# Nine of 49 first-stage products move into the edge steps, and the gathers start from normalised rows

## What is computed

```python
xn = layernorm(x)
support = segment_sum(edge_weight[:, None] * xn[src], dst)       # one sum per row
x = x + (support @ gnn_weight + gnn_bias) + linear_attention(xn) # k, v, q of xn, 8 heads
x = x + ffn(layernorm(x))                                        # gated, a mean over all rows, last norm
```

## Time and profile before

| | |
|---|---|
| median of 3 runs | 1573.97 us |
| the profiled execution's own time | 1572.78 us |
| its span, first to last instruction | 1570.8 us |
| first gather starts | 203.46 us |
| last of 784 gathers starts | 1200.69 us |
| last stage begins (its first statistics) | 1210.01 us |
| busy share of the span: PE, DVE, ACT, POOL (page, part 1) | 86%, 63%, 41%, 56% |
| mean granted clock of TensorE | 0.949 |

### The profile page before, as it was taken

How to read it: one execution, slowest core, us unless ns; L and a number is a source line. 1 busy time by engine, 2 the same in 40 slices (tenths; PEclk the granted TensorE clock), 3 DMA queues, 4 the chain that set the end, 5 groups by cost and what they waited for, 6 DMA issues and landing times. The chain is left out here.

```text
span 1570.8 us, 25004 instructions
## 1 busy us (share of the span) xinstructions
PE 1352.6 (86%) x7963; PEld 612.1 (39%) x7963; DVE 983.2 (63%) x2019; ACT 646.6 (41%) x1045; POOL 875.8 (56%) x908
## 2 busy tenths in 40 slices
PE   4989978989888897997888988899897799889994
PEld 2544423333333333443333434433343244464441
DVE  7978733334434444486756657777797777266887
ACT  4787722222222222132323323333343466327774
POOL 1000367777777777677777777777774000016763
PEclk9999989999999999899989999999999799989997
DMA  6989778888888889677777777778775988633442
GB/s 218 312 299 346 259 233 269 273 262 275 262 265 261 279 266 309 177 244 230 237 230 237 235 231 237 229 234 261 230 237 149 247 204 216 168 134 126 175 174 100
DMA packets 201552, 366.46 MB, mean 233 GB/s; under 512 B 77100, under 2 KB 82878, under 8 KB 201440
## 3 DMA queue, kind: packets, MB, share of 16 engines
q0 software_dynamic: 62720, 205.57, 42.8%
q1 hardware_dynamic: 138000, 158.43, 31.4%
q10 hardware_dynamic: 720, 1.06, 0.2%
HBM read 287.93 MB, written 65.38 MB: 225 GB/s over the span
## 5 line engine op out<-in xcount | busy, mean ns | idle before, releaser
L1167 POOL DMA_INDIRECT rows<-y_rows,idxT x516 | 495.7, 961 | 176.1 <-issue 166.6
L919 ACT ACTIVATE mb<-bank,ones,ncols 128x512 f32<-128x512 f32 x98 | 76.3, 779 | 439.2 <-PE bank L1979 439.2
L1535 DVE SCALAR_TENSOR_TENSOR acc<-bank,maskt,acc 128x512 f32 x196 | 138.0, 746 | 108.5 <-PE bank L2087 89.0
L2075 PE MATMUL bank<-rows,hots 128*32 128x512 f16 x1548 | 118.3, 413 | 67.4 <-DMA rows<-y_rows,idxT 64.6
L1979 PE MATMUL bank<-Wg,xtb 128*128 128x512 f16 x588 | 139.0, 388 | 15.6 <-DVE xtb L1469 7.9
L1979 PE MATMUL bank<-ztg,G 128*128 128x512 f16 (+1 forms) x624 | 133.5, 377 | 15.4 <-DMA ztg<-zhigh 15.1
L1979 PE MATMUL bank<-KVP,qT 128*128 128x512 f16 x588 | 143.7, 397 | 0.0
L1979 PE MATMUL bank<-Wk,xta 128*128 128x512 f16 x588 | 139.4, 388 | 0.0
L1979 PE MATMUL bank<-Wq,xta 128*128 128x512 f16 x588 | 137.2, 384 | 0.0
L2059 PE MATMUL bank<-xr,kh 128*128 128x512 f16 x392 | 124.2, 400 | 2.3 <-DVE kl L1562 2.3
L1555 DVE SCALAR_TENSOR_TENSOR kf<-bank,cols,mb 128x512 f32<-128x512 f32 x49 | 36.7, 749 | 134.3 <-ACT mb L922 134.3
(11 more groups left out here) (316 smaller groups left out, 2425.6 us busy)
## 6 DMA issues: line engine op xcount, KB each, us to landing
xta<-xt_rows SPq DMA_DIRECT2D x98, 256.0 KB, 4.1
x_rows<-xhl SPq DMA_DIRECT2D x49, 256.0 KB, 3.6
xt_rows<-xtb SPq DMA_DIRECT2D x49, 256.0 KB, 3.7
y_rows<-yb SPq DMA_DIRECT2D x49, 256.0 KB, 3.5
xr<-x_rows SPq DMA_DIRECT2D x49, 256.0 KB, 4.0
zt_rows<-ztg SPq DMA_DIRECT2D x49, 256.0 KB, 2.3
acc<-in_x SPq DMA_DIRECT2D x48, 256.0 KB, 4.1
xd<-zt_rows SPq DMA_DIRECT2D x12, 1024.0 KB, 5.5
```

What stands on the lines that cost most here:

```text
L919: nc.scalar.activation(mb[:, :], of[:, :], ACT.Relu, scale=ncols[:, col:col + 1], bias=ones[:, 0:1]).then_inc(f_min, 1)
L1167: pool.indirect_dma_start(out=row_slot(s, k).rearrange("p a d -> p (a d)"), out_offset=None, in_=y_rows, in_offset=bass.IndirectOffsetOnAx ...
L1535: nc.vector.scalar_tensor_tensor(out=flat(acc, tile + m), in0=edge_bank(n)[:, :], scalar=maskt[:, m, n:n + 1], in1=flat(acc, tile + m), op ...
L2075: ins = nc.tensor.matmul(edge_bank(n)[W * k:W * k + W, :], hots[:, r, p, :, hot_column(s, k)], row_slot(s, k)[:, q, :], start=s == FIRST[n ...
```

## The change

1. **Nine y products move.** `EARLY` is tiles 6 to 45: their 40 products stay in the head, one tick later than before (tick t+3, and their splitting in tick t+5 instead of t+3). The products of tiles 0 to 5 and 46 to 48 are made from `xt_rows`, loaded back into `xta`, in slots -6 to 0 (`Y_FIRST` = -6): two each in slots -6 and -1, one in each of the others. PE runs eight of them before its part of slot 0. They have two buffers `ylate` and four banks.
2. **The first group gathers normalised rows.** `XG` = 1: the 16 slots of group 0 gather from `x_rows`; the sum is turned instead of placed, split (`agg_higher`, `agg_lower`) and multiplied with `Wg16` (`weigh`, 12 matmuls). POOL waits before slot 0 for x_rows, xt_rows and the 40 early y stores, and for all y stores only before slot 16.
3. **Homes.** `xtb` has four buffers instead of two. `rows_v` goes: `xr`, `kh`, `kl` lie there now, since `Wg16` must live longer. `rows_p` lies over the raw `Wq`, which is now split in slots 8 to 10, so it opens only at slot 16 (`PLACES_AT`). Gathered rows have 3 homes for slots 0 to 15 and 4 up to `TURN` - 7, where there were 5.
4. **Weights.** The largest value, scale and split of `gnn_w` move from ahead of tick 0 to ticks 1, 3 and 5 to 7; the splits of `Wk` and `Wq` move out of ticks 38 to 42 into slots -4 to -2 and 8 to 10. `pack_edges` moves from ticks 33 to 39 to the loads of k tiles 8 to 14.
5. **The attention's places.** k starts in slot 3 (before -2), `TURN` is 86 (81), q starts in slot 91 (86) and takes 6 tiles in 12 slots (13), so that the last q product is in slot 187 (190). `GATE_AT` stays 165.

The core of the diff:

```diff
+G_LARGEST_AT, G_SCALE_AT, G_HIGH_AT, G_LOW_AT = 1, 3, 5, 6
-K_FIRST, K_NUM, K_DEN = -2, 10, 6
+XG = 1
+XSTEPS = sum(LONG[:XG])
+AGG = 2.0 ** -27
+PLACES_AT, WEIGHTS_AT = 16, (-4, 8)
+EARLY = list(range(6, 46))
+Y_ORDER = EARLY + [t for t in range(T) if t not in EARLY]
+NEARLY, NLATE = len(EARLY), T - len(EARLY)
+Y_FIRST, Y_NUM, Y_DEN, Y_BANKS = -6, 5, 6, 4
+K_FIRST, K_NUM, K_DEN = 3, 10, 6
-Q_FIRST, Q_NUM, Q_DEN = TURN + 5, 13, 6
+Q_FIRST, Q_NUM, Q_DEN = TURN + 5, 12, 6
...
 def row_homes():
-    free, homes = list(range(RING + 2)), []
+    free, homes = list(range(RING)), []
     for s in range(NGR):
+        if s == PLACES_AT:
+            free.insert(0, RING)
...
-            sp.wait_ge(bias_spread, 16 * 3)
-            sp.wait_ge(q_spread, 16 * 3)
+            head_ticks(head_stores, T + 2)
+            for i in range(4):
+                sp.wait_ge(head.turned_kept[i], 16 * ((T + 3 - i) // 4))
...
             def load_turned(n, t):
                 b = n % 2
-                at_least(sp, f_done, n - 1)
+                if n > 1:
+                    sp.wait_ge(y_made, min(NEARLY + n - 1, T))
+                at_least(sp, f_done, n - NLATE - 1)
...
+            for i in range(NEARLY, T + 2):
+                if i < T:
+                    load_turned(i - NEARLY, Y_ORDER[i])
+                if i >= NEARLY + 2:
+                    keep_y(i - 2)
...
-            pool.wait_ge(edges_packed, 16 * 7)
             head_kept(pool)
-            pool.wait_ge(y_made, T)
             for s in range(NGR):
+                if s == XSTEPS:
+                    for b in range(2):
+                        pool.wait_ge(y_kept[b], 16 * ((T + 1 - b) // 2))
...
+            def y_product(i):
+                n = i - NEARLY
+                b = n % 2
+                pe.wait_ge(xt_in[b], 16 * (n // 2) + 16)
+                at_least(pe, y_low, max(NEARLY, i - Y_BANKS + 1))
+                accumulate(y_bank(i)[:, :], [(xta[:, b, p, c, :], Wg16[:, q, c, :]) for c in range(C) for p, q in PASSES]
+                           ).then_inc(y_made, 1)
...
                 if s != NGR - 1:
                     place(s - 1)
                 else:
                     part(s)
+                weigh(s - 3)
+                for t in y_slots(s):
+                    y_product(t)
```

More of the change, by code:

```diff
@@ L67 @@
 U_HOT = 4
-H_HIGH, H_LOW = 3 + 2 * C, 2 + 2 * C
+H_HIGH, H_LOW = 3 + 2 * C, 3 + 2 * C
 OUTSIDE = float(1 << 20)
@@ L104, in row_homes @@
         home = free.pop(0)
-        while home in (RING, RING + 1) and s >= KEYS_END or home == RING + 3 and s >= GATE_AT:
+        while home == RING and s >= KEYS_END or home == RING + 3 and s >= GATE_AT:
             home = free.pop(0)
@@ L377, in __init__ @@
                     self.turned_in = [sem(f"{name}_turned_in{b}") for b in range(2)]
-                self.turned_kept = [sem(f"{name}_turned_kept{b}") for b in range(2)]
+                self.turned_kept = [sem(f"{name}_turned_kept{b}") for b in range(4 if name == "head" else 2)]
                 self.six = sem(name + "_six")
@@ L467, in exists, with y_slots, y_bank, y_home @@
             return not isinstance(g, int) or 0 <= tile_at(g, j) < T
+        def y_slots(s):
+            return [NEARLY + i for i in range(NLATE) if Y_FIRST + Y_NUM * i // Y_DEN == s]
+        def y_bank(i):
+            return bank[4 + i % 2] if i < NEARLY else bank[i % Y_BANKS]
+        def y_home(i):
+            return (yearly if i < NEARLY else ylate)[:, i % 2]
+        def early_at(at):
+            return EARLY.index(at) if at in EARLY else None
+        def early_before(t):
+            return sum(e <= t for e in EARLY)
         def k_slot(t):
@@ L487, in head_kept @@
         def head_kept(eng):
-            for b in range(2):
-                n = 16 * ((T + 1 - b) // 2)
-                eng.wait_ge(head.turned_kept[b], n)
-                eng.wait_ge(y_kept[b], n)
             for i in range(4):
+                eng.wait_ge(head.turned_kept[i], 16 * ((T + 3 - i) // 4))
                 eng.wait_ge(x_kept[i], 16 * ((T + 3 - i) // 4))
+            for i in range(2):
+                eng.wait_ge(y_kept[i], 16 * ((NEARLY + 1 - i) // 2))
         def late(g, j):
@@ L872, in head_tick @@
                     act.wait_ge(head.turned, t + 1)
-                    at_least(act, y_made, t - 1)
-                    at_least(act, head.turned_kept[1], 16 * half_at(g1, j1))
-                    nc.scalar.copy(xtb[:, 1], turned16(7)).then_inc(odd_out, 1)
+                    at_least(act, head.turned_kept[t % 4], 16 * (t // 4))
+                    at_least(act, y_made, early_before(t - 4))
+                    nc.scalar.copy(xtb[:, t % 4], turned16(7)).then_inc(odd_out, 1)
                 at = tile_at(g, j)
@@ L957, in kv_rows @@
                                          ).then_inc(kvp_out, 1)
-            act.wait_ge(y_low, T)
+            act.wait_ge(head.low, T)
             act.wait_ge(pool_set, 22)
-            for s in range(K_FIRST, SLOTS_END):
+            for s in range(Y_FIRST, SLOTS_END):
+                for t in y_slots(s - 1):
+                    y_higher(t)
+                if s == WEIGHTS_AT[0]:
+                    weight_high(1, Wk16, Wkraw)
+                if s == WEIGHTS_AT[1]:
+                    weight_high(2, Wq16, Wqraw)
+                n = ending(s - 2)
+                if n is not None and n < XG:
+                    agg_higher(n)
                 for slot_of, after, work in ((k_slot, 1, k_feature), (q_slot, 1, q_feature), (k_slot, 2, k_higher),
@@ L1550, in k_whole @@
                 b = t % 2
+                if t < 2:
+                    for i in range(2):
+                        dve.wait_ge(y_kept[i], 16 * ((T + 1 - i) // 2))
                 dve.wait_ge(f_exp, t + 1)
@@ L1688, in _ @@
             dve.wait_ge(pool_set, 22)
-            for s in range(K_FIRST, SLOTS_END):
-                n = ending(s - 2)
-                if n is not None:
+            for s in range(Y_FIRST, SLOTS_END):
+                for t in y_slots(s - 1):
+                    y_lower(t)
+                for k, w16, raw in ((1, Wk16, Wkraw), (2, Wq16, Wqraw)):
+                    if WEIGHTS_AT[k - 1] < s <= WEIGHTS_AT[k - 1] + 2:
+                        weight_low(k, w16, raw, low_made, s - WEIGHTS_AT[k - 1] - 1, 2)
+                n = ending(s - 2)
+                if n is not None and n < XG:
+                    agg_lower(n)
+                if n is not None and n >= XG:
+                    add_group(n, tile_at_group(n))
+                n = ending(s - 5)
+                if n is not None and n < XG:
                     add_group(n, tile_at_group(n))
```

227 lines of the change are left out of this document (129 added, 98 removed).

## The result

The changed kernel took 1582.85 us, the median of 20 runs (1576.32 to 1589.19), beside 1571.59 us for the kernel before in the same series (20 runs): a ratio of 1.0067, 95% interval 1.0052 to 1.0081. It is slower, by some 11 us. A second series of the same kernel gave 1.0051 (1.0031 to 1.0070). My 1575 us named the likeliest case as "nothing measurable"; the time lies inside the range of 1563 to 1586, and what came is nearest to the rival in which the head gains little. The profiled execution of the changed kernel took 1589.19 us (span 1587.4), the highest of its runs, so its trace shows more loss than the medians do.

A forecast was written before the change was run, and what follows sets the result against it. POOL's gather issue was taken to bound the edge steps, no single engine the head. From 1572.8 us, -15.6 (head) + 14.7 (first wait) + 0.5 + 0.5 + 2.0 = +2.1 gave 1574.9, predicted as 1575 us, range 1563 to 1586.

The forecast's parts named there:

- nothing measurable: Likeliest case for the whole kernel: the head's gain becomes POOL's wait for the first home, both some 15 us; chance 0.41.
- the rival in which the head gains little: Head: later ticks keep 3.5 us each, so the gain is 8 us instead of 15.6, total 1582 us; chance 0.16.
- What bounds the kernel: Edge steps: POOL's gather issue, 1.25 us apart, sets the pace and cannot make up for a wait; no single engine limits the head.
- Part 1, ticks 0 to 11: Start of the head: DVE's edge-list wait and load keep the gain small, 3 us at tile 11.
- After tile 48's low part: End of the head up to the first gather: 9.3 us instead of 14.1, a gain of 4.8 us.
- Part 1, ticks 11 to 48: Main part of the head: 3.35 us a tick instead of 3.56, 7.8 us gained, ends 2 and 16.
- Part 2, POOL's first wait: Before the 13th gather: eight y products delay PE's part of slot 0, costing 14.7 us; bounds 10 and 22.
- Part 3: Behind the first wait: 0.5 us in slots 3 to 15, 0.5 for repacking, 2.0 for the q stage, `TURN` unchanged.
- the late-q rival: From slot 165 on: PE at 95% of POOL's pace makes POOL wait 9 to 10 us, total 1583; chance 0.17.
- `TURN`: Around that slot: homes, key products and waits keep their places to one another, so POOL's 6.4 us wait stays.
- The weighing: Whole kernel, chances: nothing measurable 0.41, faster 0.26, late q 0.17, small head gain 0.16.
- the signs I had named: First gather at 184 to 191, one 10 to 20 us wait before the 13th, no `xtb` store waits, `TURN` wait 6 us.

The follow-up runs named there:

- experiment 2: Changed kernel with the late y products spread over slots -2 to 3, four instead of eight before slot 0, k and all behind three slots later; 1567.65 us, 0.9984.
- Experiment 1: Changed kernel with the split of y one tick after its product instead of two; 1578.66 us, ratio 1.0045.
- experiment 4: Changed kernel with both edits: split of y one tick after its product, and late y products in slots -2 to 3; 1563.09 us, ratio 0.9957.
- experiment 9: Kernel of experiment 4 with four buffers instead of two for the split y of the head; 1562.41 us, ratio 0.9922.
- experiment 10: Kernel of experiment 9 with four banks instead of two for the products of tiles 22 to 45; 1557.23 us, ratio 0.9904.
- experiment 8: Kernel before with the q pace alone changed, 6 tiles in 12 slots instead of 13; 1575.46 us, ratio 1.0011.
- experiment 7: Changed kernel with four banks instead of two for the products of tiles 22 to 45, split of y left two ticks behind; 1581.04 us, ratio 1.0043.
- experiment 6: Kernel of experiment 5 with twelve late y products instead of nine (tiles 43 to 45 late too), k one slot later; 1574.05 us, ratio 0.9993.
- Experiment 3: Kernel before with the changed kernel's homes alone: three for slots 0 to 15, a fourth from slot 16; 1573.47 us, ratio 1.0008.
- experiment 5: Kernel of experiment 4 with the late y products one slot later, slots -1 to 4, two before slot 0; 1565.43 us, ratio 0.9933.

## Why the prediction was partly right

Where the time went, by stretches between gathers, from two traces of each kernel:

| stretch | before | changed | difference of means | predicted |
|---|---|---|---|---|
| to the first gather | 203.5, 204.8 | 195.2, 195.2 | -8.9 | -15.6 |
| first to 13th gather | 15.4, 15.5 | 29.5, 30.4 | +14.5 | +14.7 |
| 13th to 57th (slots 3 to 13) | 56.8, 56.6 | 59.3, 57.3 | +1.6 | +0.5 |
| 57th to 337th (k stage) | 358.3, 362.2 | 360.8, 359.4 | -0.1 | +0.5 |
| 337th to 393rd (around `TURN`) | 76.6, 72.9 | 82.2, 83.2 | +8.0 | 0 |
| 393rd to the last (q stage) | 490.3, 491.4 | 489.6, 490.5 | -0.9 | +2.0 |
| last gather to the end | 370.1, 367.6 | 370.9, 366.7 | 0.0 | 0 |

The two spans differ by 14.2 us in the mean of these traces, by 16.6 in the first two, and the medians by 11.3 and 8.5 us.

- **What bounds the kernel** was right. POOL's gathers follow each other at 1.25 us in every kernel here, and none made up for a wait: 8.9 us more or less before the 13th gather (experiment 2) is at least that much at the end.
- **Part 1, ticks 0 to 11**: 4.5 us gained for 3 predicted. **After tile 48's low part**: 3.9 for 4.8. Both near. (The four pieces of the second add up to 9.0 us, not to the 9.3 used; measured were 10.2.)
- **Part 1, ticks 11 to 48: the step that failed.** I took 3.35 us a tick, between the old pace and PE's floor, and 7.8 us gained; measured 3.57 and nothing. I counted each engine's load and the buffers that the change adds, and not the tick more that it puts between the product and its split while the product's banks stay two. Experiment 1 gave 5.1 us for that tick alone; on experiment 4 four buffers for y gave 2.2 more (experiment 9), and four banks from tile 22 on another 1.4, beside 1.3 that no edit explains (experiment 10). At 122.0 us the ticks then pass my 124. So the pace I predicted was within reach of the engines, and the change as written did not open the way. The row was there to be read: ACT waited 7.8 us for `yb` to be stored with the split one tick behind the product.
- **Part 2, POOL's first wait**: 14.4 us for 14.7, the 13th gather 29.5 us after the first for 30.1. Of its parts, the two cold products took 6.7 us for 9, and the other six 3.2 each (19.4 us from 204.20 to 223.59), as taken; between the two lay a wait of 0.95. That the mean of 3.2 held is partly luck: two products took 8.1 and 7.6 us while their loads ran beside gathers, and 5.9 and 5.5 later, where I had 5.7 to 7.1 throughout. The 0.2 us of waking up in that term stands in no run by itself. My estimate by the Trainium skill, DMA: Bandwidth & Descriptors, section Anatomy of one DMA, was a wait of 11 us, from 2.6 us for a load of 256 KB. The trace shows 4.5 and 5.3 us while POOL gathered, 4.8 just after, and at most 2.7 later, once it stood still. The last agrees with the fit, though the fit is for a DMA of the gpsimd path and SyncE issues these; where the wait is made, the row of part 6 was the better guide, and still short.
- **Part 3.** Slots 3 to 13 cost 1.6 us in the table; for slots 3 to 15 I had 0.5, ends 0 and 3. The q stage cost nothing instead of 2, in the changed kernel and alone (experiment 8); the late-q rival falls with it. A PE at 95% of POOL's pace was enough because a part that waits only for data leaves half of the homes' time in hand.
- **`TURN`** was taken as unchanged, because homes and key products "keep their places to one another". In four traces it shows 8 us more. With those of experiments 8, 1 and 7 as well, the stretch takes 72.9, 76.6 and 79.0 us in kernels with the slots and homes of before, and 76.6, 79.3, 82.2 and 83.2 with the changed ones: 4.2 us between the means, with a scatter as large, which is in part the clock's. Some 3 us of it belong to the change, as the traces show at one place. There the groups have two slots, so PE places a group's sum in every second slot only. With `TURN` 81 it is not in slot `TURN`; with 86 it is. DVE then adds the group's sum to `acc` (1.4 us) before it copies the sum of the keys (`ksb`), and PE waits for that copy (first the changed kernel, then the kernel before):

```profile
674.90 1.05 PE L2239 MATMUL bank<-ones,ksb 1*128 1x1 f32 x8 [1.49 <-DVE ksb L1697]
676.22 2.75 PE L2247 MATMUL bank<-ident,M 128*128 128x128 f32 x16 [0.27 <-DVE M L1707]
```

```profile
634.88 1.05 PE L2137 MATMUL bank<-ones,ksb 1*128 1x1 f32 x8
```

  The 16 matmuls behind the wait run in part at the lower level (mean clock 0.68), 2.75 us instead of 1.97. From PE's sum of the keys to the end of the next part the same work takes 9.7 us instead of 6.6. The wait of 1.5 us is in all five traces with `TURN` at 86 or 90 (the changed kernel's two, experiments 1, 7 and 6: 9.7 to 9.9 us) and in none of the nine with 81 or 89, experiment 2's among them. No experiment moved `TURN` alone, and what else of the 8 us belongs to the change stays open. Experiment 3 (80.8) would put it to the homes, but its trace has four groups of small matmuls at or near the lower level that the others have at full pace (up to 2.08 us each instead of 1.16), and its median is only 1.5 us up. With 3 us for `TURN` the sum is 9.2 us, where the medians say 11.3 and 8.5.
- **The weighing.** That the head would gain little had a chance of 0.16 and a time of 1582. I set "the waits on `xtb` go for certain" against it; they went, and their time went into other waits. That this rival's 1582 meets the measured time is partly luck: it counts nothing for `TURN`, and 2 us for the q stage that were not lost. Of the signs I had named, the long wait before the 13th gather came, and so did the end of the waits on `xtb`; the first gather (195.2) lay outside 184 to 191, and the wait near `TURN` did not stay at 6.

## What to carry to other kernels

When a change puts a step one tick later in a pipeline, count the buffers and banks on both of its sides against the new distance, before counting loads; waits that are deleted elsewhere say nothing about the tick. When work is moved by some slots, look what else each of its new slots holds: five slots put `TURN` on one with a placing, for some 3 us. Where an issue queue has a fixed pace and no way to catch up, whatever starts it earlier is worth only what stands ready for it: here 8.9 us earlier were paid back with 14.5, because eight products stood before the first part that frees a home. A wait table names the last link of a chain: where PE had waited 8.1 us for the split, four banks took the whole wait away and the ticks became 1.4 us shorter. And before a gain is put down to an edit, look whether it lies where the edit can act: half of the 2.7 us that the four banks seemed to give in experiment 10 does not.

## What the runs showed of the hardware

- Loads of 256 KB issued while POOL gathered took 4.5 and 5.3 us, one issued 1.2 us behind its last gather 4.8, and one issued 8.9 us behind it at most 2.7. With two buffers these loads were most of what PE waited for in the first slots (12.9 of 20.4 us in experiment 5), though PE was busy only 56 of 77 us.
- Where PE had stood idle for 1.8 us at `TURN` (two waits, 1.49 and 0.27 us), the 16 small matmuls behind took 2.75 us at a mean clock of 0.68; in the kernel before, without the waits, they took 1.97. In the four other traces with these waits they took 2.7 to 3.4.
- The granted clock fell while PE had hardly a gap, and not at the same row in each execution. Over the stretch before the long wait at `TURN` PE was busy 10.82 of 10.90 us at a mean clock of 0.77 in the first line below, the changed kernel's; in experiment 7, the second, 8.90 of 9.00 us at 0.94.

```profile
688.50:699.40 10.90, 10.82 (x16) 2.77 (x16) 0.22 (x2) 0.55 (x1) 3.78 (x4) 0.77 0.34 98
```

```profile
685.50:694.50 9.00, 8.90 (x16) 2.36 (x16) 0.23 (x2) 0.56 (x1) 4.29 (x5) 0.94 0.61 178
```
